# Turning tiles on TensorE by halves of the rows instead of whole, in the local-attention stage of a fused transformer kernel

## The chip, the cores and the metric

The kernel runs on one core of a Trainium2 chip. The metric is the device time of one execution in microseconds, lower being better; of the kernel before three executions were timed.

## The reference, cut to what matters

The program is two small transformer layers and a third part, a local-attention transformer of depth 6, on an input of 4 batches of 512 tokens with 128 features. The first two parts take the first 606 us and aren't touched. The third part is this, for each of its 6 layers:

```python
def attn_layer(x, Wqkv, qs, ksc, Wo):            # 16 heads of 64, window 32
    q, k, v = split(x @ Wqkv)                     # 128 -> 3 * 1024
    q = l2norm(q) * qs;  k = l2norm(k) * ksc      # per head
    q = q * cos * scale + rotate_half(q) * sin * scale
    k = k * cos / scale + rotate_half(k) * sin / scale
    out = local_attention(q, k, v)                # each window of 32 sees itself and the one before
    return out.reshape(b, n, 1024) @ Wo

for i in range(6):
    x = attn_layer(shift_tokens(x), ...) + x
    x = ffn_layer(shift_tokens(x), ...) + x       # layer norm, 128 -> 2 * 341, gelu gate, 341 -> 128
```

In the local attention a query block of 32 tokens meets 64 keys; the scores times 8 are masked, go through a softmax, and weigh 64 rows of v.

## The kernel before, in words

All engines run their own instruction streams and meet at semaphores. The third part walks over tiles of 128 tokens: 6 layers, 4 batches, 4 tiles t = 0 to 3 of a batch, 96 tiles in all. Every engine has a function `slot` that is called once per tile and writes out by hand what the engine does in it; the order on the engine is the order in that function. A slot holds three tiles in different stages: tile g is projected, tile g-1 is turned and scored, tile g-2 is weighted.

On TensorE (`slot`, line 1065) the order is: two query products (`project` 0 and 1, three matmuls of 128x512 each), `turn_q`, key product 2, `probs`, key product 3, values 0, `turn_k`, values 1, value product 4, scores 0, value product 5, scores 1, `out_`. Beside that come parts of the output projection and the feed-forward of earlier batches, by t: in t = 0 the first feed-forward matmuls ahead of `turn_q` and the first half of the output projection (`wo_half`, 16 matmuls with 256 columns) behind it; in t = 1 the second feed-forward matmuls (`ff_down`, line 1167) behind `turn_q`; in t = 2 the second half of the output projection ahead of `turn_q`; in t = 3 a layer norm's turn behind values 1.

The turns are what the change is about. TensorE turns (transposes) the normalised, rotated queries and keys (`ra`), the exponentials (`Ex`) and the weighted values (`On`), each an array of 128 tokens by 1024 columns, in eight blocks of 128 columns, a pair of heads each. A block is a matmul with the data as weights and the identity matrix streaming past them: 128 rows, 128 weight columns, 128 streamed columns. Blocks 0 to 3 go to the first bank of `tr` in PSUM, blocks 4 to 7 to the second (`turn`, `turn_probs`, `turn_out`, lines 1004 to 1025). After every four blocks a semaphore (`qk_tr`, `e_tr`, `on_tr`) tells ScalarE, which copies the bank into SBUF (`take_qk_part`, `take_probs`, `take_out`, lines 2141 to 2165; the profile shows all ScalarE work at line 1924 and all turns at line 589) and counts up `qk_cp`, `pt_cp` or `o_cp`. So the first copy can run while the second four blocks are turned.

Who waits for the copies: scores 0 and values 0 take pairs 0 to 3, so they wait for the first copy of the keys or probabilities (`qk_cp` at `g * 4 + 3`, `pt_cp` at `g * 2 + 1`, lines 1030 and 1046), scores 1 and values 1 for the second. The next turn writes the same banks, so its first four blocks wait for the first copy of the turn before, its second four for the second one. `window_scores` and `values` work with tiles of 64 rows and 32 columns, the two heads of a pair on the two row halves and the four windows on the four column groups, into the two banks of `sc` or `oo` (lines 1027 to 1058).

On VectorE a slot begins, behind the softmax of the tile before, with the rotation of the query products (lines 1729 and 1731), which frees the bank for key product 2. On ScalarE a slot is two squares, the exponential, the query copies (with a gelu between them in t = 0), a square, the probability copies (with a shifted copy of the input between them in t = 1 of most batches), a square, in t = 2 a shifted copy, the mask, the key copies, the value copies, inverse roots, and the output copies (`slot`, line 2172). ScalarE turns to each when it comes to it in that order.

Of the kernel before, what the change touches and what calls it, by code (L numbers as in the profile page):

```python
# [109 lines left out]
def build(nc, ins, out):  # L110
    ctx = ExitStack()
    with ctx:
# [471 lines left out]
        def _(pe):  # L584
# [427 lines left out]
            def turn_probs(g, j):  # L1012

                for u in range(4):
                    pr = 4 * j + u
                    last = tp(tr[:, j, u * P:(u + 1) * P], Ex[:, 2 * pr:2 * pr + 2, :])
                last.then_inc(e_tr, 1)

            def turn_out(g, j):

                pe.wait_ge(on_ok, g + 1)
                for u in range(4):
                    pr = 4 * j + u
                    last = tp(tr[:, j, u * P:(u + 1) * P], On[:, pr * P:(pr + 1) * P])
                last.then_inc(on_tr, 1)
# [39 lines left out]
            def slot(s_):  # L1065
# [10 lines left out]
                def turn_q():  # L1076
                    for j in range(2):
                        if g >= 3:
                            pe.wait_ge(o_cp, (g - 3) * 2 + j + 1)
                        elif g == 2:  # L1080
                            pe.wait_ge(qk_cp, 3 + j)
                        turn(g - 1, t - 1, j)

                def turn_k():
                    for j in range(2):
                        if d_:
                            pe.wait_ge(pt_cp, (g - 2) * 2 + j + 1)
                        else:
                            pe.wait_ge(qk_cp, (g - 1) * 4 + j + 1)
                        turn(g - 1, t - 1, 2 + j)  # L1090

                def probs():
                    pe.wait_ge(e_exp, g - 1)
                    for j in range(2):
                        if c_:
                            pe.wait_ge(qk_cp, (g - 1) * 4 + j + 1)
                        else:
                            pe.wait_ge(o_cp, (g - 3) * 2 + j + 1)
                        turn_probs(g - 2, j)
# [12 lines left out]
                def out_():  # L1112
                    for j in range(2):
                        if c_:
                            pe.wait_ge(qk_cp, (g - 1) * 4 + j + 3)
                        else:
                            pe.wait_ge(pt_cp, (g - 2) * 2 + j + 1)
                        if t == 0 and m2 is not None:
                            pe.wait_ge(ff_ev, m2 * FFC + 2)
                        if t == 3 and j == 0 and m1 is not None:  # L1120
                            pe.wait_ge(lnb_out, m1 + 1)
                        turn_out(g - 2, j)
# [121 lines left out]
            def drain():  # L1244

                for j in range(2):
                    pe.wait_ge(o_cp, (TZ - 2) * 2 + j + 1)
                    turn(TZ, T - 1, j)
# [4 lines left out]
                for j in range(2):  # L1253
                    pe.wait_ge(qk_cp, TZ * 4 + j + 1)
                    turn_probs(TA, j)
                values(NB - 1, TA, T - 2, 0)
                for j in range(2):
                    pe.wait_ge(pt_cp, TA * 2 + j + 1)
                    turn(TZ, T - 1, 2 + j)
# [3 lines left out]
                for j in range(2):  # L1263
                    pe.wait_ge(qk_cp, TZ * 4 + j + 3)
                    turn_out(TA, j)
# [3 lines left out]
                for j in range(2):  # L1269
                    pe.wait_ge(o_cp, TA * 2 + j + 1)  # L1270
                    turn_probs(TZ, j)
# [5 lines left out]
                for j in range(2):  # L1277
                    pe.wait_ge(pt_cp, TZ * 2 + j + 1)
                    turn_out(TZ, j)
# [642 lines left out]
        def _(ac):  # L1922
# [232 lines left out]
            def take_probs(g, j):  # L2155
# [3 lines left out]
                act(PT[:, 4 * j:4 * j + 4, :], tr[:, j].rearrange("p (a b) -> p a b", b=P), ACT.Copy  # L2159
                    ).then_inc(pt_cp, 1)  # L2160

            def take_out(g, t, j):
                ac.wait_ge(on_tr, g * 2 + j + 1)
                act(oT[:, 4 * j:4 * j + 4, t * P:(t + 1) * P], tr[:, j].rearrange("p (a b) -> p a b", b=P),
# [7 lines left out]
            def slot(s_):  # L2172
# [17 lines left out]
                if c_:  # L2190
                    take_qk_part(g - 1, (t - 1) % T, 0)
                if t == 0 and m2 is not None:
                    gelu(m2, 0, FFB[0])
                    log_exp_tables()
                if c_:
                    take_qk_part(g - 1, (t - 1) % T, 1)
# [16 lines left out]
                if d_:  # L2213
                    take_probs(g2, 1)
# [222 lines left out]
```

## Time and profile before

| | |
|---|---|
| median of three executions | 2197.93 us (2195.68 to 2202.28) |
| span of the profiled execution, first to last instruction | 2182.5 us |
| TensorE busy | 2005.7 us, 34395 matmuls |
| VectorE, ScalarE, POOL busy | 1809.4, 1579.9, 1167.3 us |
| stage of the tiles | from 606 us to the end |
| DMA packets of the program, share of 16 engines | 22.0% |

For the profiled execution the profile gives the span; the timed executions hold what lies around it as well, 15.4 us by the median. A matmul's time in the profile is modelled and runs from its issue to its last result, so the starts tell more than the sums. In the timeline, instructions of the same kind in a row are one line: the start of the first, the time from that to the end of the last, and their count.

### The profile page before, as it was taken

The page shows a single profiled execution, that of the slowest core. Times are in us where ns is not written, and L with a number is a line of the kernel's source. Part 1 is how long each engine was busy: PE and PEld are TensorE (multiplying, and loading weights), DVE is VectorE, ACT ScalarE, POOL GpSimd, SP SyncE. Part 2 cuts the span into 40 slices and gives each one's busy share as a digit, 9 for nine tenths or more (in the row PEclk, how much of TensorE's full clock was granted, in tenths as well). Part 3 has the DMA queues.
Part 4 walks back from the last instruction along what each step waited for, and adds up shares of the span by engine and source line. Part 5 has one row for each costly group of instructions (what it writes and reads, how often), then busy time and mean ns, then how long its engine had stood idle before and what let it go on. Part 6 is the DMA issues. An engine that isn't in the chain of part 4 may idle for free.

```text
span 2182.5 us, 82607 instructions
## 1 busy us (share of the span) xinstructions
PE 2005.7 (92%) x34395; PEld 1457.7 (67%) x34395; DVE 1809.4 (83%) x3751; ACT 1579.9 (72%) x3031; POOL 1167.3 (53%) x1413
## 2 busy tenths in 40 slices
PE   6888899987699999999999999999999999999997
PEld 4666654455577776777777777777767777677775
DVE  7888765678798998888988888988888988888884
ACT  4777753365577887787877788777787878887773
POOL 1112110000577676666776667666667767667761
PEclk9999999998899999999999999999999999999999
DMA  4000001000122232222322223322232322332221
GB/s 114 1 2 2 2 31 59 30 1 30 52 72 68 61 105 69 68 63 71 90 72 75 66 58 95 81 68 66 70 87 71 87 58 58 102 82 62 75 59 40
DMA packets 98196, 132.18 MB, mean 61 GB/s; under 512 B 27900, under 2 KB 42882, under 8 KB 97826
## 3 DMA queue, kind: packets, MB, share of 16 engines
q1 hardware_dynamic: 97826, 126.90, 22.0%
q8 instruction: 275, 4.51, 0.8%
q14 instruction: 95, 0.78, 0.1%
HBM read 28.20 MB, written 1.11 MB: 13 GB/s over the span
## 4 chain that ended last, share of the span: by engine, by line
PE 72%; DVE 13%; issue 6%; ACT 6%; POOL 1%; SPq 1%; DMA 0%; DVEq 0%; POOLq 0%; ACTq 0%
PE oo L586 21%; PE pj L586 19%; PE tr L589 14%; PE sc L586 13%; ACT arena L1924 3%; PE tr L586 2%; DVE arena L1729 2%; DVE xn L1318 2%; DVE arena L1486 1%; PE oo L589 1%; DVE arena L1731 1%; DVE arena L1750 1%; DVE arena L1752 1%; PE sc L589 1%; ACT sc L1924 1%
## 5 line engine op out<-in xcount | busy, mean ns | idle before, releaser
L2345 POOL TENSOR_TENSOR arena<-arena 128x1024 f32<-128x1024 f32 x192 | 456.9, 2380 | 336.9 <-DVE arena L1731 336.9
L1924 ACT ACTIVATE arena<-tr 128x512 f32<-128x512 f32 (+2 forms) x874 | 460.8, 570 | 111.9 <-PE tr L589 109.7
L1924 ACT ACTIVATE arena<-pj 128x512 f32<-128x512 f32 x576 | 341.7, 599 | 189.5 <-PE pj L586 150.4
L589 PE MATMUL tr<-ident,arena 128*128 128x128 f32 x2882 | 413.3, 279 | 25.3 <-DMA beta<-in_L_attn_betas 9.8
L1924 ACT ACTIVATE arena<-arena 128x16 f32<-128x16 f32 (+6 forms) x808 | 362.3, 454 | 98.7 <-DVE arena L1486 74.0
L589 PEld LDWEIGHTS tr<-ident,arena 128*128 128x128 f32 x2882 | 330.6, 141 | 93.4 <-issue 34.5
L2363 POOL TENSOR_TENSOR arena<-arena 128x1024 f32<-128x1024 f32 x192 | 366.7, 1910 | 23.2 <-POOL arena L2356 0.9
L1729 DVE TENSOR_TENSOR arena<-pj,rtab 128x512 f32<-128x512 f32 x384 | 259.8, 677 | 24.8 <-ACT arena L1924 23.4
L586 PE MATMUL oo<-slab,arena 64*32 64x64 f32 (+1 forms) x12416 | 232.1, 228 | 41.0 <-issue 26.4
L1731 DVE TENSOR_TENSOR arena<-pj,rtab 128x512 f32<-128x512 f32 x384 | 261.4, 681 | 0.0
L1737 DVE TENSOR_REDUCE arena<-arena 128x8 f32<-128x512 f32 x384 | 255.6, 677 | 0.0
L586 PEld LDWEIGHTS oo<-slab,arena 64*32 64x32 f32 (+1 forms) x12416 | 158.3, 106 | 123.7 <-issue 94.7
L586 PE MATMUL pj<-w_lo,xs_hi 128*128 128x512 f32 x576 | 227.5, 395 | 0.1
L586 PEld LDWEIGHTS sc<-arena 64*32 64x32 f32 x12288 | 136.0, 105 | 91.0 <-issue 75.0
L586 PE MATMUL sc<-arena 64*32 64x64 f32 x12288 | 171.7, 224 | 6.8 <-issue 5.5
L2312 POOL TENSOR_SCALAR rstd<-mv 128x4 f32<-128x4 f32 x40 | 11.4, 284 | 294.3 <-DVE mv L1312 292.2
L1750 DVE TENSOR_REDUCE arena<-sc 128x16 f32<-128x1024 f32 x96 | 117.2, 1220 | 38.5 <-PE sc L586 38.5
L1770 DVE TENSOR_TENSOR slab<-oo,arena 128x1024 f32<-128x1024 f32 x96 | 117.1, 1220 | 18.3 <-PE oo L586 16.2
L1486 DVE CUSTOM_DVE_ANT_0 arena<-pj,biases 128x128 f32<-128x128 f32 (+3 forms) x214 | 101.1, 486 | 24.3 <-PE pj L586 23.2
L586 PEld LDWEIGHTS pj<-w_lo,xs_hi 128*128 128x128 f32 x576 | 110.1, 191 | 16.4 <-issue 12.2
L1752 DVE TENSOR_TENSOR arena<-sc,arena 128x1024 f32<-128x1024 f32 x96 | 117.5, 1224 | 3.3
L1761 DVE TENSOR_REDUCE arena<-arena 128x16 f32<-128x1024 f32 x96 | 116.3, 1212 | 1.0 <-ACT arena L1924 1.0
(289 smaller groups left out, 3802.5 us busy)
## 6 DMA issues: line engine op xcount, KB each, us to landing
slab<-arena SPq DMA_DIRECT2D x576, 128.0 KB, 2.4
slab<-arena SPq DMA_DIRECT2D x336, 64.0 KB, 2.0
wqkv<-in_L_ffn_Wqkv SPq DMA_DIRECT2D x18, 512.0 KB, 4.2
arena<-gate_mem SPq DMA_DIRECT2D x24, 256.0 KB, 4.3
wo<-in_L_ffn_Wo SPq DMA_DIRECT2D x6, 512.0 KB, 4.2
w<-in_L_ffn_W SPq DMA_DIRECT2D x6, 341.0 KB
YT<-in_L_attn_x SPq DMA_DIRECT2D x4, 256.0 KB, 3.5
arena<-in_L_ffn_W SPq DMA_DIRECT2D x1, 1024.0 KB
```

The source lines that it names most:

```text
L586: return nc.tensor.matmul(o, l, r, start=start, stop=stop, **k)
L589: return nc.tensor.transpose(o, i, ident[0:i.shape[0], 0:i.shape[0]])
L1486: v.tensor_tensor_reduce(out=Ssb[:, n % 4, 0:w], in0=SBANK[n % 3][:, 0:w], in1=bias[:, S - w:S], scale=-1.0, scalar=3e38, op0=ALU.add, op1 ...
L1729: v.tensor_tensor(ra[:, t % 2, k, co].rearrange("p (h u d) -> p h u d", u=2, d=DL // 2), src, tc_.unsqueeze(1).broadcast_to(wide), ALU.mult)
L1731: v.tensor_tensor(rb[:, k, co].rearrange("p (h u d) -> p h u d", u=2, d=DL // 2), src[:, :, ::-1, :], ts_.unsqueeze(1).broadcast_to(wide), ...
L1737: v.tensor_reduce(ss[:, k, hf * PAIRS:(hf + 1) * PAIRS, 0], sq[:, c % 2].rearrange("p (h d) -> p h d", d=DL), AX.X, ALU.add).then_inc(ss_o ...
L1750: v.tensor_reduce(mx, s_v, AX.X, ALU.max).then_inc(mx_ok, 1)
L1752: v.tensor_tensor(Tm.rearrange("p (a u) b -> p u a b", u=2), sc[:, :, :].rearrange("p u (a b) -> p u a b", b=2 * WIN), mx.rearrange("p (u ...
L1770: v.tensor_tensor(On.rearrange("p (a u d) -> p u a d", u=2, d=DL), oo[:, :, :].rearrange("p u (a d) -> p u a d", d=DL), ri.rearrange("p (a ...
L1924: return nc.scalar.activation(o, i, f, **k)
L2345: p_.tensor_tensor(r_, r_, rb[:, k, :], ALU.add).then_inc(sum_ok, 1)
L2363: p_.tensor_tensor(r3, r3, rs[:, k, :].unsqueeze(2).broadcast_to([P, HL, DL]), ALU.mult).then_inc(qk_rdy, 1)
```

## The change

A turn is no longer eight blocks of 128 rows but sixteen of 64 rows: for each pair of heads one block takes tokens 0 to 63 into the first bank of `tr`, the next one tokens 64 to 127 into the second. Each has 64 rows, 128 weight columns and 64 streamed columns. A bank then holds all eight pairs of one half of the tokens, and ScalarE's two copies go by halves of the tokens instead of halves of the pairs; their size is the same. The waits of TensorE become one per turn, for the later copy; values 0 and scores 0 wait for both copies. On ScalarE the second copy of the queries now stands directly behind the first, ahead of the gelu of t = 0, and the second copy of the probabilities directly behind the first, ahead of the shifted copy of t = 1 and, once a layer, the conversion of weights. The function `drain` for the last tiles is changed in the same way.

```diff
-            def turn(g, t, j):
-                pe.wait_ge(qk_rdy, g * 2 + j // 2 + 1)
-                for u in range(4):
-                    pr = 4 * (j % 2) + u
-                    last = tp(tr[:, j % 2, u * P:(u + 1) * P], ra[:, t % 2, j // 2, pr * P:(pr + 1) * P])
-                last.then_inc(qk_tr, 1)
...
+            def turn_rows(rows, done):
+                for pr in range(PAIRS):
+                    for u in range(2):
+                        r = slice(u * DL, (u + 1) * DL)
+                        last = nc.tensor.transpose(tr[:, u, pr * DL:(pr + 1) * DL], rows(r, pr), ident[r, r])
+                        if pr == PAIRS - 1:
+                            last.then_inc(done, 1)
+
+            def turn(g, t, k):
+                pe.wait_ge(qk_rdy, g * 2 + k + 1)
+                turn_rows(lambda r, pr: ra[r, t % 2, k, pr * P:(pr + 1) * P], qk_tr)
+
+            def turn_probs():
+                turn_rows(lambda r, pr: Ex[r, 2 * pr:2 * pr + 2, :], e_tr)
+
+            def turn_out(g):
                 pe.wait_ge(on_ok, g + 1)
+                turn_rows(lambda r, pr: On[r, pr * P:(pr + 1) * P], on_tr)

             def window_scores(g, t, i):
-                pe.wait_ge(qk_cp, g * 4 + 3 + i)
                 if i == 0:
+                    pe.wait_ge(qk_cp, g * 4 + 4)
                     pe.wait_ge(masked, g + 1)
...
             def values(n, g, t, i):
-                pe.wait_ge(pt_cp, g * 2 + 1 + i)
+                pe.wait_ge(pt_cp, g * 2 + 2)
...
                 def turn_q():
-                    for j in range(2):
-                        if g >= 3:
-                            pe.wait_ge(o_cp, (g - 3) * 2 + j + 1)
-                        elif g == 2:
-                            pe.wait_ge(qk_cp, 3 + j)
-                        turn(g - 1, t - 1, j)
+                    if g >= 3:
+                        pe.wait_ge(o_cp, (g - 2) * 2)
+                    elif g == 2:
+                        pe.wait_ge(qk_cp, 4)
+                    turn(g - 1, t - 1, 0)
...
                 def probs():
                     pe.wait_ge(e_exp, g - 1)
-                    for j in range(2):
-                        if c_:
-                            pe.wait_ge(qk_cp, (g - 1) * 4 + j + 1)
-                        else:
-                            pe.wait_ge(o_cp, (g - 3) * 2 + j + 1)
-                        turn_probs(g - 2, j)
+                    if c_:
+                        pe.wait_ge(qk_cp, (g - 1) * 4 + 2)
+                    else:
+                        pe.wait_ge(o_cp, (g - 2) * 2)
+                    turn_probs()
...
             def take_qk_part(g, t, j):
                 ac.wait_ge(qk_tr, g * 4 + j + 1)
-                src = tr[:, j % 2].rearrange("p (a b) -> p a b", b=P)
-                pr = slice(4 * (j % 2), 4 * (j % 2) + 4)
-                dst = qT[:, pr, :] if j < 2 else kT[:, pr, WIN + t * P:WIN + (t + 1) * P]
+                src = tr[:, j % 2].rearrange("p (a b) -> p a b", b=DL)
+                at = j % 2 * DL
+                dst = qT[:, :, at:at + DL] if j < 2 else kT[:, :, WIN + t * P + at:WIN + t * P + at + DL]
                 act(dst, src, ACT.Copy).then_inc(qk_cp, 1)
...
                 if c_:
                     take_qk_part(g - 1, (t - 1) % T, 0)
+                if c_:
+                    take_qk_part(g - 1, (t - 1) % T, 1)
                 if t == 0 and m2 is not None:
                     gelu(m2, 0, FFB[0])
                     log_exp_tables()
-                if c_:
-                    take_qk_part(g - 1, (t - 1) % T, 1)
...
                 if d_:
                     take_probs(g2, 0)
+                    take_probs(g2, 1)
                 if s_.ahead is not None and t == 1:
...
-                if d_:
-                    take_probs(g2, 1)
```

`turn_k` and `out_` change as `turn_q` does, `take_probs` and `take_out` as `take_qk_part`.

## Rows read from the trace of the kernel before

**Rows 1.** The page: busy time by engine, and the chain that ended last.
```profile
PE 2005.7 (92%) x34395; PEld 1457.7 (67%) x34395; DVE 1809.4 (83%) x3751; ACT 1579.9 (72%) x3031; POOL 1167.3 (53%) x1413
...
PE 72%; DVE 13%; issue 6%; ACT 6%; POOL 1%; SPq 1%; DMA 0%; DVEq 0%; POOLq 0%; ACTq 0%
```

**Rows 2.** Busy time by engine in the tile stage; then clock, DMA share, GB/s.
```profile
606.00:2150.00 1544.00, 1467.22 (x30311) 1108.26 (x30312) 1342.32 (x2234) 1217.58 (x2242) 1063.97 (x1268) 1.00 0.28 74
```

**Rows 3.** Groups by line and shape on TensorE, from 606 us: busy, mean ns, idle before.
```profile
L589 PE MATMUL tr<-ident,arena 128*128 128x128 f32 x2264 | 301.7, 276 | 4.3 <-POOL arena L2363 2.5 <-ACT arena L1924 1.8
...
L586 PE MATMUL oo<-slab,arena 64*32 64x64 f32 x12160 | 169.4, 224 | 40.7 <-issue 26.2 <-DVE xn L1318 13.6 <-ACT arena L1924 1.0
...
L586 PE MATMUL pj<-wk_hi,xs_hi 128*128 128x512 f32 x186 | 94.4, 507 | 13.7 <-DVE arena L1731 13.7
```

**Rows 4.** Timeline of TensorE in a slot of t = 2: start, length, matmuls, count.
```profile
1514.90 1.04 PE L589 MATMUL tr<-ident,arena 128*128 128x128 f32 x8
1515.69 0.48 PE L586 MATMUL pj<-wk_hi,xs_hi 128*128 128x512 f32 x1
...
1516.24 0.39 PE L586 MATMUL pj<-wk_hi,xs_lo 128*128 128x512 f32 x1
1516.47 1.03 PE L589 MATMUL tr<-ident,arena 128*128 128x128 f32 x8
...
1517.81 0.40 PE L586 MATMUL pj<-wk_hi,xs_lo 128*128 128x512 f32 x1
1518.13 0.86 PE L586 MATMUL oo<-slab,arena 64*32 64x64 f32 x64
1518.92 1.09 PE L589 MATMUL tr<-ident,arena 128*128 128x128 f32 x8
1519.95 0.86 PE L586 MATMUL oo<-slab,arena 64*32 64x64 f32 x64
...
1521.78 0.25 PE L586 MATMUL sc<-arena 64*32 64x64 f32 x3
```

**Rows 5.** Timelines of ScalarE and of TensorE in a slot of t = 0.
```profile
1544.40 0.60 ACT L1924 ACTIVATE arena<-tr 128x512 f32<-128x512 f32 x1 [0.55 <-PE tr L589]
...
1544.64 3.62 PE L586 MATMUL sc<-arena,wo 128*128 128x256 f32 x16
```

**Rows 6.** Timeline of ScalarE in the slot of rows 4 (t = 2).
```profile
1515.53 1.09 ACT L1924 ACTIVATE arena<-tr 128x512 f32<-128x512 f32 x2 [2.29 <-PE tr L589]
...
1517.22 1.08 ACT L1924 ACTIVATE arena<-tr 128x512 f32<-128x512 f32 x2
...
1518.79 1.26 ACT L1924 ACTIVATE xcur<-YT 64x512 f32<-64x512 f32 x2
1520.08 1.03 ACT L1924 ACTIVATE sc<-wmask 128x1024 f32<-128x1024 f32 x1
1521.13 1.08 ACT L1924 ACTIVATE arena<-tr 128x512 f32<-128x512 f32 x2
```

**Rows 7.** Timeline of all engines where a slot of t = 1 begins.
```profile
1493.77 1.28 ACT L1928 ACT_TABLE_LOAD   x1
...
1495.43 1.07 ACT L1924 ACTIVATE arena<-tr 128x512 f32<-128x512 f32 x2
...
1496.07 1.14 PE L589 MATMUL tr<-ident,arena 128*128 128x128 f32 x8
```

**Rows 8.** Timeline of all engines in a slot of t = 3.
```profile
1527.72 1.05 ACT L1924 ACTIVATE arena<-arena 128x1024 f32<-128x1024 f32 x1
...
1528.60 0.50 PE L586 MATMUL pj<-wk_hi,xs_hi 128*128 128x512 f32 x1 [0.59 <-DVE arena L1731]
1528.67 1.08 ACT L1924 ACTIVATE arena<-tr 128x512 f32<-128x512 f32 x2
...
1529.40 1.07 PE L589 MATMUL tr<-ident,arena 128*128 128x128 f32 x8
...
1531.66 0.57 PE L586 MATMUL oo<-slab,arena 64*32 64x64 f32 x35 [0.51 <-DVE xn L1318]
```

More of the change, by code:

```diff
@@ L1002, in project @@
                 mm(pj[:, c % 2], xs_lo[:, x_], w_hi[k][:, w_], start=False).then_inc(pj_mm, 1)
-            def turn(g, t, j):
-                pe.wait_ge(qk_rdy, g * 2 + j // 2 + 1)
-                for u in range(4):
-                    pr = 4 * (j % 2) + u
-                    last = tp(tr[:, j % 2, u * P:(u + 1) * P], ra[:, t % 2, j // 2, pr * P:(pr + 1) * P])
-                last.then_inc(qk_tr, 1)
[L1012 to L1019, printed above, removed]
+            def turn_rows(rows, done):
[11 more added lines that the diff above has]
+            def turn_out(g):
                 pe.wait_ge(on_ok, g + 1)
[L1022 to L1025, printed above, removed]
+                turn_rows(lambda r, pr: On[r, pr * P:(pr + 1) * P], on_tr)
             def window_scores(g, t, i):
-                pe.wait_ge(qk_cp, g * 4 + 3 + i)
                 if i == 0:
+                    pe.wait_ge(qk_cp, g * 4 + 4)
                     pe.wait_ge(masked, g + 1)
@@ L1076, in turn_q @@
                 def turn_q():
-                    for j in range(2):
-                        if g >= 3:
-                            pe.wait_ge(o_cp, (g - 3) * 2 + j + 1)
-                        elif g == 2:
-                            pe.wait_ge(qk_cp, 3 + j)
-                        turn(g - 1, t - 1, j)
-                def turn_k():
-                    for j in range(2):
-                        if d_:
-                            pe.wait_ge(pt_cp, (g - 2) * 2 + j + 1)
-                        else:
-                            pe.wait_ge(qk_cp, (g - 1) * 4 + j + 1)
-                        turn(g - 1, t - 1, 2 + j)
+                    if g >= 3:
[3 more added lines that the diff above has]
+                    turn(g - 1, t - 1, 0)
+                def turn_k():
+                    if d_:
+                        pe.wait_ge(pt_cp, (g - 1) * 2)
+                    else:
+                        pe.wait_ge(qk_cp, (g - 1) * 4 + 2)
+                    turn(g - 1, t - 1, 1)
                 def probs():
                     pe.wait_ge(e_exp, g - 1)
-                    for j in range(2):
-                        if c_:
-                            pe.wait_ge(qk_cp, (g - 1) * 4 + j + 1)
-                        else:
-                            pe.wait_ge(o_cp, (g - 3) * 2 + j + 1)
-                        turn_probs(g - 2, j)
+                    if c_:
+                        pe.wait_ge(qk_cp, (g - 1) * 4 + 2)
+                    else:
+                        pe.wait_ge(o_cp, (g - 2) * 2)
+                    turn_probs()
                 def values_(i):
@@ L1112, in out_ @@
                 def out_():
-                    for j in range(2):
-                        if c_:
[L1115 to L1122, printed above, removed]
+                    if c_:
+                        pe.wait_ge(qk_cp, g * 4)
+                    else:
+                        pe.wait_ge(pt_cp, (g - 1) * 2)
+                    if t == 0 and m2 is not None:
+                        pe.wait_ge(ff_ev, m2 * FFC + 2)
+                    if t == 3 and m1 is not None:
+                        pe.wait_ge(lnb_out, m1 + 1)
+                    turn_out(g - 2)
                 def wo_half(m, i):
@@ L1244, in drain @@
             def drain():
-                for j in range(2):
-                    pe.wait_ge(o_cp, (TZ - 2) * 2 + j + 1)
-                    turn(TZ, T - 1, j)
+                pe.wait_ge(o_cp, (TZ - 1) * 2)
+                turn(TZ, T - 1, 0)
                 pe.wait_ge(v_cp, TZ * 2 + 2)
@@ L1252, in drain @@
                 pe.wait_ge(e_exp, TA + 1)
-                for j in range(2):
-                    pe.wait_ge(qk_cp, TZ * 4 + j + 1)
-                    turn_probs(TA, j)
+                pe.wait_ge(qk_cp, TZ * 4 + 2)
+                turn_probs()
                 values(NB - 1, TA, T - 2, 0)
-                for j in range(2):
-                    pe.wait_ge(pt_cp, TA * 2 + j + 1)
-                    turn(TZ, T - 1, 2 + j)
+                pe.wait_ge(pt_cp, TA * 2 + 2)
+                turn(TZ, T - 1, 1)
                 values(NB - 1, TA, T - 2, 1)
@@ L1262, in drain @@
                 window_scores(TZ, T - 1, 1)
-                for j in range(2):
-                    pe.wait_ge(qk_cp, TZ * 4 + j + 3)
-                    turn_out(TA, j)
+                pe.wait_ge(qk_cp, TZ * 4 + 4)
+                turn_out(TA)
                 final(0)
@@ L1268, in drain @@
                 pe.wait_ge(e_exp, TZ + 1)
-                for j in range(2):
-                    pe.wait_ge(o_cp, TA * 2 + j + 1)
-                    turn_probs(TZ, j)
+                pe.wait_ge(o_cp, TA * 2 + 2)
+                turn_probs()
                 pe.wait_ge(f_cp, 2)
@@ L1276, in drain @@
                 ff_up(MY, 1, LAST_FF[MY][1])
-                for j in range(2):
-                    pe.wait_ge(pt_cp, TZ * 2 + j + 1)
-                    turn_out(TZ, j)
+                pe.wait_ge(pt_cp, TZ * 2 + 2)
+                turn_out(TZ)
                 last_out_project(0)
@@ L2158, in take_probs @@
                     wait(ac, o_mm, g)
-                act(PT[:, 4 * j:4 * j + 4, :], tr[:, j].rearrange("p (a b) -> p a b", b=P), ACT.Copy
+                act(PT[:, :, j * DL:(j + 1) * DL], tr[:, j].rearrange("p (a b) -> p a b", b=DL), ACT.Copy
                     ).then_inc(pt_cp, 1)
@@ L2163, in take_out @@
                 ac.wait_ge(on_tr, g * 2 + j + 1)
-                act(oT[:, 4 * j:4 * j + 4, t * P:(t + 1) * P], tr[:, j].rearrange("p (a b) -> p a b", b=P),
+                act(oT[:, :, t * P + j * DL:t * P + (j + 1) * DL], tr[:, j].rearrange("p (a b) -> p a b", b=DL),
                     ACT.Copy).then_inc(o_cp, 1)
@@ L2191, in slot @@
                     take_qk_part(g - 1, (t - 1) % T, 0)
+                if c_:
+                    take_qk_part(g - 1, (t - 1) % T, 1)
                 if t == 0 and m2 is not None:
@@ L2212, in slot @@
                     weights_high(l, 2)
-                if d_:
-                    take_probs(g2, 1)
                 if new:
```

1 line of the change is left out of this document (removed).

## The prediction

> **What bounds the kernel now.** The page comes first. TensorE is busy 92% of the span and the chain of work that ended last lies on it for 72%, with VectorE next at 13% [rows 1]. The busy table of the tile stage alone (606 to 2150 us) says the same more sharply: TensorE 1467 of 1544 us, VectorE 1342, ScalarE 1218, the granted clock 1.00, which is the upper of its two levels, 2.4 GHz, throughout [rows 2]. The groups by line say what TensorE waits for in that stage: in the values it stands still for 26.2 us that the profile can't put down to anybody and for 13.6 us on a layer norm's `xn`, before the first key product 13.7 us on VectorE's rotation, and before the turns almost nothing [rows 3]. So a tile is a queue of TensorE work with small holes, and what counts is what is added to that queue or taken from it. A tile has four turns (queries, probabilities, keys, output). With 6 layers, 4 batches and 4 tiles there are 96 tiles, 24 of each t, and t matters since other work is slotted in beside the turns.
>
> **Part 1, the turns themselves.** Eight turns of 128x128 take 1.04 us, the modelled time of one being 0.27, so they start (1.04-0.27)/7 = 0.110 us apart [rows 4]. Behind a window product the same eight take 1.09: the first one's weight load of 0.055 is no longer under the work ahead of it. Hence of one turn's 0.110 the load takes 0.055 and the streaming of 128 columns the other 0.055, one after the other.
>
> The new form is 16 turns of 64 rows with 64 streamed columns each. No row shows a 64-row, 128-column tile. The nearest is the window product, 64x32, on eight tiles: 64 of them in 0.86 us [rows 4]. What one column costs there comes from 16 products of 256 columns in 3.62 us [rows 5]: starts (3.62-0.38)/15 = 0.216 apart, 0.38 being an estimate of one's time from the 0.39 of the rows beside it [rows 4]. So each window product has a load of 0.216 x 32/256 = 0.027 and a stream of 0.054 us, 0.081 together, and eight in turn on each of the eight tiles make 0.65, which is what the group takes up to its last start (0.86 less the 0.22 of one [rows 3]). So there the two row halves do stream together, and most loads overlap too. I therefore take the halves as working side by side: eight times 0.055+0.027 = 0.082 us each, first to last start 0.57 against 0.77: **-0.20 us** a turn. Bounds: if a load of half the rows, or a stream, were all there is (0.055 apart on each half), 0.39, so -0.38; if the loads of both halves follow one another, 15 x 0.055 = 0.83, so +0.06.
>
> A rule speaks against the saving. The Trainium skill, "TensorE: Matmul & The Clock Gate", section "LDWEIGHTS (loading the stationary operand)", says that a load goes by its columns and not by its rows. The halved turns then load twice as many columns in all; by it each load stays at its full price, which the sum has, and it leaves open whether two run at once, which is the second rival.
>
> **Part 2, the change of shape.** The product ahead of the values (64x32) starts at 1517.81, and the values 0.32 later, where a turn, of the same shape, comes after 0.23 (1516.24, 1516.47); with its load now exposed that is 0.09+0.055 = **0.15 us** for going in. Coming out, a turn's modelled end lies 0.25 behind the start of the product that follows it (1514.90+1.04 against 1515.69) but only 0.06 behind the start of the values (1518.92+1.09 against 1519.95): 0.19, less the shorter last stream, **0.17 us** [rows 4]. The turn of keys has values on both sides and already pays, and the output's pays going in. Queries, probabilities (both ways) and output (out) are new: five changes of shape in a tile. These two prices are for a change of rows and columns together; the trace has no change of rows alone, so the bounds are 0 and 0.15 / 0.17. I take the upper end, the only row there is.
>
> Here a rule of the Trainium skill decides: "TensorEngine Tiling (Array Packing)", section "Key Properties", says that a change of tiling mode, though not of tile, drains TensorE. By it the upper end holds; without it the sum would be 20 and not 51 us.
>
> **Part 3, the copies.** This is the largest part. Both banks are now filled only at the end of a turn, ScalarE copies one bank after the other, and whoever follows on TensorE needs both copies: values and scores read all pairs over both halves of the tokens, and the next turn writes both banks. Until now the first copy ran under the second half of the turn, and the follower needed the first copy alone. A copy starts about 0.30 us after the start of the matmul that it waits for (the fourth starts at 1514.90+0.33 = 1515.23, the copy at 1515.53 [rows 6]), 0.28 with the shorter stream. The two take 1.09, and TensorE goes on 0.04 later (one copy takes 0.60 [rows 5], and 1495.43+0.60 stands against 1496.07 [rows 7]). New rule: **last start of a turn + 1.41 us**.
> - Probabilities to values: now 1518.13-1517.23 = 0.90 [rows 4], the last start of a turn being its own start plus 1.03 less 0.27; +0.51, in t = 0, 1, 2. A change of shape on the way is inside.
> - Queries to probabilities where one product alone lies between (t = 2): now 1516.47-1515.67 = 0.80 [rows 4], +0.61. In t = 3 the copies run behind the exponential and end at 1528.67+1.08, so the probabilities start at 1529.79 and not 1529.40 [rows 8]. In t = 0 the products of 3.62 us [rows 5] and in t = 1 the feed-forward's second matmuls (line 1167) cover the copies; if that cover went, the +0.61 would be there too.
> - Scores in t = 2: between the probabilities' copies and the keys' copies ScalarE has a square, a shift of 1.26 and the mask of 1.03, from 1517.22+1.08 to 1521.13+1.08 = 3.91 us, while the scores start 3.65 behind the values, on the first copy [rows 4, 6]. They must now wait for the second: +0.26, and the shorter turn of keys saves nothing in front of it.
> - Output to queries, t = 0 into 1: ScalarE is held by a table load, copies at 1495.43 for 1.07, so queries at 1496.54 and not 1496.07: +0.47, with the turn's saving and both changes of shape inside [rows 7].
>
> The two copies that move on ScalarE (the second query copy ahead of a gelu, the second probability copy ahead of the shifted input) delay those by 0.6 us at most; the gelu feeds a gate on VectorE, which the query product of 3.62 us hides. Sizes and layouts of the copies stay, so their 1.09 for two does. SyncE's and POOL's orders aren't touched.
>
> **The sum**, over one set of four tiles. Into t = 1: +0.47. Into t = 2 and into t = 0: output -0.20, out 0.17, in 0.15, so +0.12 each. Into t = 3: nothing, as TensorE waits 0.59 for VectorE in front of the key product [rows 8]. Inside t = 0 and t = 1: three turns -0.60, out 0.17, in 0.15, values +0.51, so +0.23 each. Inside t = 2: two turns -0.40, +0.61, +0.51, +0.26 = +0.98. Inside t = 3: the probabilities' last start is 1529.79+0.055+0.57 = 1530.42, the values follow at 1531.83 and not 1531.66, +0.17, and keys -0.20: -0.03. Together 2.12 us, times 24 = **+51 us**. The profiled execution spans 2182.5 us, so 2233 is expected there; the median of the runs, 2197.93, lies 15 us above that span, which the change doesn't touch: 2249.
>
> **The rivals.**
> - *A change of rows alone doesn't drain.* Then in t = 0, in t = 1, into t = 2 and into t = 0 each lose 0.32: 1.28 x 24 = 31 us less, +20, 2218. For it: every drain in the trace goes with a change of columns. Chance 0.16.
> - *The loads of the halves follow one another.* A turn costs +0.06 instead of -0.20 at the 12 turns of the set that the sum counts: 0.26 x 12 x 24 = +75, so +126, 2324. Against it: 64 window loads of 0.027 would need 1.7 us and take 0.65, though four column groups alone could explain this. Chance 0.20.
> - *Faster.* The place is the spacing on one half. If in half-row tiles the load of the next turn runs under the stream of this one, the spacing is 0.055, a turn saves 0.38, another 0.18 x 12 x 24 = 52 us; without drains that gives 20-52 = -32, 2166. It decides once a turn saves more than 0.20+0.07 = 0.27 us and the drains are free (20/(12 x 24) = 0.07). Against it: today load and stream of a turn stand in line, 0.110. Chance 0.11.
> - *TensorE's lost time is swallowed* by the unexplained pauses in the values (26.2 us [rows 3]), up to half of the 51: 2223, within the range, counted in the forecast's share.
>
> **How the numbers follow.** The forecast has 0.53, the rivals 0.16, 0.20 and 0.11. The prediction is the likeliest case, 2249. The range reaches from below the first rival (2210) to the second (2325); what it leaves out is the faster case and the upper part of the second. A measurement tells 0.3%, 6.6 us, from no change. Faster 0.12; the same 0.05, out of the first rival's and the faster one's edges; slower 0.83.
>
> **What would show it.** In the profile after: the turns' tile form 64*128 with twice the count; a turn's 16 in 0.57 first to last start (0.83 for the second rival, 0.39 for the faster one). The gap from a product to a turn 0.32 and not 0.23, or the first rival holds. ScalarE's two copies in one piece behind every turn, the values 1.41 after the probabilities' last start, and TensorE waits on ScalarE in front of values, probabilities and scores where there are almost none now, some 0.5 us each. Wrong it is if those waits are there and the time isn't, or if TensorE's wait for VectorE's rotation grows instead.

## The result, and the profile after

The changed kernel takes 2240.7 us (median of four executions, 2228.7 to 2246.0) and the kernel before 2199.45 on the same chip: ratio 1.0183, 95% interval 1.0152 to 1.0215, 41 us slower. The forecast was 51 us, 2249.

The page of the changed kernel: spans and busy time, the chain, and three groups.

```profile
span 2244.2 us, 88464 instructions
...
PE 1966.2 (88%) x37467; PEld 1362.4 (61%) x37467; DVE 1801.5 (80%) x3751; ACT 1569.3 (70%) x3031; POOL 1166.4 (52%) x1413
...
PE 64%; DVE 14%; ACT 12%; issue 8%; POOL 1%; SPq 1%; DMA 0%; DVEq 0%; POOLq 0%; ACTq 0%
...
L1009 PE MATMUL tr<-ident,arena 64*128 64x64 f32 x4608 | 205.2, 228 | 32.5 <-ACT arena L1914 28.1
...
L586 PE MATMUL pj<-wk_hi,xs_hi 128*128 128x512 f32 x192 | 100.0, 521 | 24.7 <-DVE arena L1721 24.7
```

TensorE is busy 39.5 us less than before and the execution 62 us longer by its span: the turns got shorter, and what came in their place is waiting. On the chain ScalarE went from 6% to 12% [rows 1]. The turns, in front of which TensorE hardly waited [rows 3], now stand 28 us behind ScalarE's copies. (The first profile of the kernel before was of an execution some 13 us quicker than its median; a second one spans 2196.4 us. The comparison below is by single stretches, and by the second pair of profiles where totals count.)

The same slot as in [rows 4] (t = 2) in the changed kernel, TensorE:

```profile
1545.44 0.71 PE L1009 MATMUL tr<-ident,arena 64*128 64x64 f32 x16
1546.09 0.51 PE L586 MATMUL pj<-wk_hi,xs_hi 128*128 128x512 f32 x1
...
1547.42 0.71 PE L1009 MATMUL tr<-ident,arena 64*128 64x64 f32 x16 [0.36 <-ACT arena L1914]
...
1549.32 0.85 PE L586 MATMUL oo<-slab,arena 64*32 64x64 f32 x64 [0.30 <-issue]
1550.10 0.71 PE L1009 MATMUL tr<-ident,arena 64*128 64x64 f32 x16
1550.74 0.86 PE L586 MATMUL oo<-slab,arena 64*32 64x64 f32 x64
```

The last line but one to [rows 4]'s 1518.92 and 1519.95: from the turn of keys to values 1 it is 0.64 us, not 1.03. But from the turn of queries to that of probabilities it is 1.98, not 1.57, and from there to the values 1.90, not 1.66: there TensorE waits for this (ScalarE, same slot; the pairs of copies are now in one piece each, in [rows 6] too, but start behind the whole turn):

```profile
1546.19 1.09 ACT L1914 ACTIVATE arena<-tr 128x512 f32<-128x512 f32 x2 [2.49 <-PE tr L1009]
...
1548.14 1.08 ACT L1914 ACTIVATE arena<-tr 128x512 f32<-128x512 f32 x2 [0.37 <-PE tr L1009]
```

### The profile page after: what moved, and what is told of

Read it like the earlier page. It is cut to its first block, busy times and chain, and to the rows that moved or that the text cites. A ratio compares the mean times of both kernels' runs of the same rounds, so it can differ in the third digit from the quotient of the medians.

```text
span 2244.2 us, 88464 instructions
## 1 busy us (share of the span) xinstructions
PE 1966.2 (88%) x37467; PEld 1362.4 (61%) x37467; DVE 1801.5 (80%) x3751; ACT 1569.3 (70%) x3031; POOL 1166.4 (52%) x1413
## 4 chain that ended last, share of the span: by engine, by line
PE 64%; DVE 14%; ACT 12%; issue 8%; POOL 1%; SPq 1%; DMA 0%; DVEq 0%; POOLq 0%; ACTq 0%
PE oo L586 21%; PE pj L586 18%; PE sc L586 11%; PE tr L1009 8%; ACT arena L1914 8%; PE tr L586 2%; PE tr L589 2%; DVE arena L1721 2%; DVE xn L1308 2%; DVE arena L1476 2%; DVE arena L1719 1%; PE oo L589 1%; ACT L1918 1%; DVE arena L1740 1%; DVE arena L1742 1%
## 5 line engine op out<-in xcount | busy, mean ns | idle before, releaser
L1914 ACT ACTIVATE arena<-tr 128x512 f32<-128x512 f32 (+2 forms) x874 | 455.2, 569 | 152.2 <-PE tr L1009 143.3
L1009 PEld LDWEIGHTS tr<-ident,arena 64*128 64x128 f32 x4608 | 167.3, 138 | 123.3 <-issue 81.7
L1009 PE MATMUL tr<-ident,arena 64*128 64x64 f32 x4608 | 205.2, 228 | 32.5 <-ACT arena L1914 28.1
L586 PEld LDWEIGHTS sc<-arena 64*32 64x32 f32 x12288 | 141.1, 108 | 119.7 <-issue 91.6
L586 PE MATMUL sc<-arena 64*32 64x64 f32 x12288 | 180.9, 230 | 27.2 <-issue 16.4
L589 PE MATMUL tr<-ident,arena 128*128 128x128 f32 x578 | 104.6, 286 | 20.8 <-DMA beta<-in_L_attn_betas 10.0
L586 PE MATMUL pj<-wk_hi,xs_hi 128*128 128x512 f32 x192 | 100.0, 521 | 24.7 <-DVE arena L1721 24.7
```

Of the source, the lines that this page charges most:

```text
L586: return nc.tensor.matmul(o, l, r, start=start, stop=stop, **k)
L589: return nc.tensor.transpose(o, i, ident[0:i.shape[0], 0:i.shape[0]])
L1009: last = nc.tensor.transpose(tr[:, u, pr * DL:(pr + 1) * DL], rows(r, pr), ident[r, r])
L1914: return nc.scalar.activation(o, i, f, **k)
```

## The experiments

Theory 1 is the forecast's: the wait for both copies costs, the shorter turns give back, the changes of shape (drains) take part of that again. Its rival puts the loss on the drains and on the 6144 added instructions (3072 loads and as many matmuls). Two more theories came up on the way.

**whole_late: the late copies alone.** `turn_rows` of the change with whole blocks, each copy taking four pairs again, all else as in the change:

```diff
-                    for u in range(2):
-                        r = slice(u * DL, (u + 1) * DL)
-                        last = nc.tensor.transpose(tr[:, u, pr * DL:(pr + 1) * DL], rows(r, pr), ident[r, r])
-                        if pr == PAIRS - 1:
-                            last.then_inc(done, 1)
+                    last = tp(tr[:, pr // 4, pr % 4 * P:(pr % 4 + 1) * P], rows(slice(0, P), pr))
+                last.then_inc(done, 2)
```

> Whole blocks of 128 rows as before, but both banks signalled only at the end of a turn, one wait for both copies, and the order of ScalarE's copies as in the change: the late copies alone. Theory 1 (the loss is the wait for both copies): 0.51 at the values in three of four tiles, 0.6 at the probabilities of t = 2, about 0.5 each in front of the queries of t = 1, the probabilities and values of t = 3 and the scores of t = 2, some 3.5 us per set of four tiles, 24 sets: 2275 to 2290 us, slower than the changed kernel, and values 1.44 us behind the last start of the probabilities' turn. Rival (the copies are hidden and the drains and the added instructions cost the time): within 10 us of the kernel before.

Measured: 2273.3 us, 1.0342 of the kernel before (1.032 to 1.0363), **77 us slower**, and 33 slower than the change itself; the 2275 to 2290 expected were just missed. The late copies are the largest term, and the shape gives back some 33 net. A slot of t = 2 in whole_late, TensorE and ScalarE:

```profile
1561.40 1.06 PE L589 MATMUL tr<-ident,arena 128*128 128x128 f32 x8 [0.57 <-ACT arena L1911]
...
1562.50 1.08 ACT L1911 ACTIVATE arena<-tr 128x512 f32<-128x512 f32 x2 [0.76 <-PE tr L589]
...
1562.77 0.40 PE L586 MATMUL pj<-wk_hi,xs_lo 128*128 128x512 f32 x1
1563.69 0.85 PE L586 MATMUL oo<-slab,arena 64*32 64x64 f32 x64 [0.52 <-issue]
```

From the product's last matmul to the values it is 0.92, where [rows 4] have 1518.13-1517.81 = 0.32. The trace books this wait as "issue", since it can't match the copy's signal; the second copy ends at 1562.50+1.08 = 1563.58, 0.11 ahead of the values, so I take it as ScalarE's. The values start 1.50 behind the turn's last start (1.44 expected).

**before_small and after_small: both kernels with small copies.** In the ninth and later tiles each copy takes a sixteenth of its elements, so most of the turned data is left out:

```diff
-                act(dst, src, ACT.Copy).then_inc(qk_cp, 1)
+                n_ = 8 if g >= 8 else None
+                act(dst[:, :, 0:n_], src[:, :, 0:n_], ACT.Copy).then_inc(qk_cp, 1)
```

(4 of 64 instead of 8 of 128 on the changed kernel; the same for `PT` and `oT`.)

> The kernel before with ScalarE's copies of the turned tiles cut to a sixteenth of their elements from the ninth tile on; it leaves out most of the turned data, and serves as the base of after_small. Theory 1: ScalarE stands behind few TensorE waits here, so little is gained, 2175 to 2200 us. Rival (ScalarE is a second bound): below 2150 us.

> The changed kernel with the same cut of the copies, most of the turned data left out: what is left of the change is the shape, five drains and the added instructions in each tile. Theory 1 (turns save 0.28 to 0.33 us each, drains cost 0.12 each): 30 to 45 us below before_small. Rival (drains and instruction loading cost more than the turns save): level with before_small or up to 40 us above it.

Measured: 2186.2 us (0.995 of the kernel before) and 2175.4 (0.9911). ScalarE is no second bound: with a fifth of its work gone the kernel gains 10 us. And with the copies out of the way the new shape is faster, by 11 us in the median (2169.6 to 2186.0 against 2184.1 to 2189.5), so the loss isn't in the shape. But 11 is about a third of the 30 to 45 that theory 1 expected. Something takes back the other 19 to 34 us.

**halves_in_turn: do the row halves run side by side?**

```diff
-                for pr in range(PAIRS):
-                    for u in range(2):
+                for u in range(2):
+                    for pr in range(PAIRS):
```

> The changed kernel with the two loops of a turn swapped: all eight blocks of the upper row half into bank 0, then the eight of the lower one into bank 1, so that two blocks in a row use the same rows. If the two halves' loads and streams run side by side in the change, a turn's first to last start goes from 0.49 to 1.0 or more, the first copy starts half a turn ahead of the end, and the time is 2245 to 2300 us. If the spacing is set by something else than the rows, the turn stays at 0.49 and the earlier copy brings the time below 2230 us.

Measured: 2282.9 us (1.0387, 1.0365 to 1.041), 42 above the change. The turn of the probabilities in a slot of t = 1, with its two copies:

```profile
1548.91 1.01 PE L1009 MATMUL tr<-ident,arena 64*128 64x64 f32 x16
...
1549.66 1.09 ACT L1914 ACTIVATE arena<-tr 128x512 f32<-128x512 f32 x2
```

It takes 1.01 and not 0.71, from first to last start 0.79 and not 0.49; 1.0 or more was expected. The single starts say why (medians over the turns of the stage, 377 and 378). In the change the sixteen blocks start as eight pairs, 3 ns apart within a pair, and from pair to pair 0.111 us once and then 0.062. In halves_in_turn the starts fall into two rows of eight of just that spacing, 0.111 and then 0.062: the first half's, and from 0.304 on the second half's, which begin while three of the first half are still to come. So eight blocks on one half take 0.484 from first to last start, and sixteen on both take 0.487: **the halves run fully side by side**. And one half alone is quicker than the 0.082 that I had added up. The first step is longer than the others by its exposed load, 0.049; with whole blocks it is 0.055 (0.164 against 0.109), so a load of half the rows costs nearly the full price. By an estimate from these, 0.062-0.049 = 0.013 us of the 0.027 of streaming is left beside the next load and the rest hides under it, where with 128 rows load and stream stand in line (0.109).

A half by itself thus takes as long as both together, and handing over the first bank early gains nothing: in both kernels the first copy starts 0.81 us behind the turn's start and the second 1.30 (medians).

**keys_halves and its companions: the half of the change that should pay.** The turn of keys has window products on both sides, so no drain is added, and over a microsecond of work lies ahead of the scores. Only this turn is halved, by the change's own loop; the scores wait for both copies. In keys_halves_mask_first ScalarE also does this in t = 2, and in before_mask_first nothing else is changed:

```diff
-                if t == 2 and m1 is not None:
-                    ac.wait_ge(y_att, m1 * 2 + 2)
-                    shifted(xsF, YT[:, s_.y1:s_.y1 + S], 0, S).then_inc(xs_f, 1)
                 if c_:
...
                     take_qk_part(g - 1, (t - 1) % T, 3)
+                if t == 2 and m1 is not None:
+                    ac.wait_ge(y_att, m1 * 2 + 2)
+                    shifted(xsF, YT[:, s_.y1:s_.y1 + S], 0, S).then_inc(xs_f, 1)
```

> The kernel before with the turn of keys alone by row halves: it has window products on both sides, so it adds no change of shape, and over a microsecond of other work lies between it and the scores. Theory 1 (turn saves 0.33, drains and late copies are what the change loses by): -0.33 in t = 0, 1 and 3; in t = 2 the scores wait for the second copy, 0.47 more, less what is saved: about -0.5 us per set, 2180 to 2192 us beside a kernel before at 2197. Rival (the added instructions alone cost more than the turns save): level or slower.

> As keys_halves, and in t = 2 ScalarE does the mask and the key copies ahead of the shifted input instead of behind it, so that the scores need not wait for the second key copy. Theory 1: -0.33 in all four tiles and the 0.15 that the scores of t = 2 waited: -1.4 us per set, 2155 to 2172 us. Rival (VectorE bounds once TensorE is shorter, its wait before the key product grows): no faster than keys_halves.

> The kernel before with that order of ScalarE alone. Theory 1: removes the 0.15 us that the scores of t = 2 waited for the first copy, some 4 us, 2190 to 2197. Rival (the order is what brings the gain and the halved turn nothing): as fast as keys_halves_mask_first.

Measured: 2222.6 us (1.0112, 1.0099 to 1.0126), 2215.2 (1.0078, 1.0058 to 1.0098) and 2198.2 (1.0001, 0.9992 to 1.0011). All three expectations of theory 1 failed: the turn of keys is 0.39 us shorter in 96 tiles, 37 us, and the kernel is 25 us *slower*. In keys_halves_mask_first TensorE's waits for ScalarE in front of the scores are 1.9 us instead of the 12.2 of keys_halves, which accounts for the 7 us between the two. Where the rest goes the trace shows. keys_halves, TensorE, early in the stage:

```profile
666.56 0.71 PE L1010 MATMUL tr<-ident,arena 64*128 64x64 f32 x16
667.20 0.72 PE L586 MATMUL oo<-slab,arena 64*32 64x64 f32 x49
669.67 0.34 PE L586 MATMUL oo<-slab,arena 64*32 64x64 f32 x15 [1.74 <-issue]
...
670.83 1.15 PE L586 MATMUL sc<-arena 64*32 64x64 f32 x64
...
673.25 0.63 PE L586 MATMUL pj<-w_lo,xs_hi 128*128 128x512 f32 x1
673.67 0.63 PE L586 MATMUL pj<-wv_hi,xs_lo 128*128 128x512 f32 x1
```

Two things. First, 1.74 us of standstill in the midst of a group whose instructions wait for nothing. Between 666.5 and 669.7 us the DMA engines carry one packet, and it is this:

```profile
q8 instruction: 1, 0.02, 2.4%
```

A packet of instructions is 16 KB (4.60 MB in 281 packets), and from pause to pause the matmuls counted in the trace are multiples of 126 or so: a packet holds 256 instructions, a load and a matmul being two. TensorE resumes a median of 2.4 to 2.6 us after such a packet starts. I read this as TensorE having run out of instructions. Second, after the pause two matmuls of 512 columns start 0.42 us apart and not 0.23. The stages by window, columns as in [rows 2]:

```profile
663.00:670.80 7.80, 6.06 (x167) 4.69 (x165) 5.62 (x11) 6.52 (x11) 4.51 (x2) 1.00 0.08 20
670.80:674.20 3.40, 3.40 (x72) 2.48 (x71) 2.51 (x10) 0.92 (x3) 1.79 (x5) 0.52 0.02 5
674.20:680.00 5.80, 5.19 (x92) 4.25 (x92) 4.95 (x9) 4.98 (x10) 4.94 (x8) 0.99 0.36 93
```

For 3.4 us the granted clock is at its lower level, 1.2 GHz; ahead of it came the turn, then the pause. The kernel before shows 1.00 in the whole stage [rows 2].

**more_instructions and the padded pair: is it the count of instructions, or how fast they are used?** Theory 2: in the stretch from values to scores TensorE uses up instructions faster than packets of them arrive. First 3072 instructions were added (the page's count goes from 82607 to 85679; I had reckoned with 6144) that do no work:

```diff
+            def passed():
+                for _ in range(8):
+                    pe.wait_ge(set_tr, 1)
```

called at the head of `turn`, `turn_probs` and `turn_out`. Then work with few instructions was added to the kernel before and to keys_halves:

```diff
+                if c >= 4:
+                    mm(pj[:, c % 2], xs_hi[:, x_], w_hi[k][:, w_])
                 mm(pj[:, c % 2], xs_hi[:, x_], w_hi[k][:, w_], stop=False)
```

> The kernel before with eight further waits on a semaphore passed long ago ahead of each half turn, 64 a tile, 6144 in all, about as many instructions as the change adds on TensorE. If the pauses in the midst of window products come from loading instructions, their total rises from some 40 us towards 60 and the time by 15 to 30 us beyond what the waits take themselves; if they come from something else, they stay at 37 to 43 us.

> The kernel before with the first matmul of each value product done once more ahead of it: two matmuls of 512 columns a tile, 0.23 us each, 4 instructions in all, 96 tiles: 44 us of streaming, in the stretch of the window products. Theory 2 (in that stretch TensorE is held by the loading of its instructions, 16 KB at a time, each 2.4 us from its start to the next instruction): part of it falls into the pauses, whose total drops from 43 towards 30 us: 2215 to 2235 us. Theory 1 alone: the pauses stay, 2235 to 2245.

> The same padding on keys_halves (2222.6 us, pauses of 84 us). Theory 2: the pauses shrink by half or more of what is added, to 40 to 60 us, and the padding costs 10 to 25 us only: 2232 to 2248 us, so that the distance to before_padded is smaller than the 25 us without padding, or gone. Theory 1 alone: the full 44 us, 2262 to 2270, the pauses staying at 84.

Measured: 2248.6 us (1.0228, 1.0213 to 1.0243), 2221.7 (1.0114, 1.0094 to 1.0134) and 2244.2 (1.0213, 1.0198 to 1.0228). The added instructions cost 51 us by themselves, but the pauses, which were to stay or to grow, shrink to 30 us: the count isn't it. (The page has 287 packets of instructions for 275, twelve more for its 3072 instructions, which is 256 in each.) The padding of 44 us costs 24 us in the kernel before and 22 in keys_halves, so half of it falls into time that was lost anyway: the pauses are 7 to 12 and 17 us shorter. That much of theory 2 holds. That the two would close up failed: they stay 22 us apart, the pauses of keys_halves_padded being 64 us and not 40 to 60.

**before_again and after_again: a second look at both.** Theory 3: with half-row turns go two costs, pauses and falls of the clock.

> The kernel before once more, for a second profile of it: its first one spans 2182.5 us, 13 less than the median. Theory 3 (two costs go with half-row turns: pauses at the loading of instructions, and falls of the granted clock to its lower level): pauses of 37 to 47 us, at most three falls of the clock between 606 us and 35 us before the end. Rival (the first two profiles differ by chance): either is as large as in the changed kernel.

> The changed kernel once more. Theory 3: pauses of 50 to 70 us and ten or more falls of the clock, 35 to 50 us at the lower level, 2235 to 2246 us. Rival: pauses and falls as in the kernel before, with the time still 40 us above it.

Measured: 2195.3 us and 2235.4 (ratio 0.9986 and 1.017, 1.0143 to 1.0197). The falls came out as theory 3 has them; the pauses of before_again, 48 us, lie just above the expected 37 to 47. All runs side by side. A pause is counted where two matmuls of one group and of fewer than 512 columns, the second waiting for nothing, start more than 0.4 us apart; a fall is a stretch at 1.2 GHz in the trace's record of the clock, from 606 us to 35 us before the end. The last column counts the standstills of TensorE of 1.3 us or more, by the ends of its matmuls, for whatever reason.

| kernel | median us | pauses, their us | falls, us at 1.2 GHz | standstills of 1.3 us and more |
|---|---|---|---|---|
| before | 2199.5 | 45, 43 | 0, 0 | 3 |
| before_again | 2195.3 | 49, 48 | 3, 10 | 8 |
| before_mask_first | 2198.2 | 46, 45 | 1, 3 | 6 |
| before_padded | 2221.7 | 34, 36 | 2, 7 | 6 |
| before_small | 2186.2 | 46, 40 | 4, 14 | 8 |
| more_instructions | 2248.6 | 36, 30 | 0, 0 | 6 |
| whole_late | 2273.3 | 39, 38 | 2, 7 | 5 |
| *half-row turns:* the change | 2240.7 | 54, 64 | 13, 48 | 22 |
| after_again | 2235.4 | 51, 56 | 11, 44 | 14 |
| after_small | 2175.4 | 65, 67 | 7, 34 | 17 |
| halves_in_turn | 2282.9 | 44, 49 | 11, 48 | 13 |
| keys_halves | 2222.6 | 68, 81 | 11, 41 | 24 |
| keys_halves_mask_first | 2215.2 | 74, 86 | 10, 44 | 18 |
| keys_halves_padded | 2244.2 | 48, 64 | 10, 41 | 24 |

The falls separate the two families without an exception, 0 to 4 against 7 to 13. The sum of the pauses doesn't explain it: halves_in_turn has the pauses of before_again and 11 falls to its 3. The single long standstills may. Each of the 85 falls has a standstill of TensorE of 1.2 to 2.9 us right beside it, one that still lasts when the clock falls or has ended at most 2.2 us before, be it a pause or a wait for another engine; and of standstills of 1.3 us and more the half-row kernels have 13 to 24, the others 3 to 8. Not each brings a fall: 68 of 132 do in the half-row kernels, 11 of 42 in the others. So whether the half-row turns count by themselves, or only through the longer standstills that come with them, no run here separates.

The views show the same where totals are given, the stretch from 606 to 2150 us of before_again and of after_again having a granted clock of 1.00 and 0.99:

```profile
606.00:2150.00 1544.00, 1461.54 (x29885) 1.00 0.28 73
```

```profile
606.00:2150.00 1544.00, 1390.80 (x32332) 0.99 0.28 72
```

The waits of TensorE in after_again and then in before_again:

```profile
PE oo L586 <- issue: 53.5, 89, 2.6
PE tr L1009 <- ACT arena L1914: 26.4, 71, 0.7
PE pj L586 <- DVE arena L1721: 22.2, 25, 1.0
...
PE sc L586 <- ACT arena L1914: 9.9, 17, 0.6
```

```profile
PE oo L586 <- issue: 28.2, 27, 2.5
PE pj L586 <- DVE arena L1731: 13.6, 23, 0.6
```

(89 "issue" waits for 27: ScalarE's late copies in front of the values are booked there, as in whole_late, beside the pauses.)

## Why the prediction was right, point by point

The time came out near, 2240.7 us for 2249, and the mechanism of the loss is the forecast's, but that the sum fits is in part luck. Interval by interval, in us from start to start, forecast and measured (after_again less before_again, medians of the 23 or 24 slots of each t, behind values 1 the lower quartile, since many pauses fall there):

| interval | t = 0 | t = 1 | t = 2 | t = 3 |
|---|---|---|---|---|
| output to queries | +0.12, -0.08 | +0.47, +0.48 | +0.12, -0.08 | 0, -0.09 |
| queries to probabilities | +0.12, -0.04 | +0.12, -0.15 | +0.41, +0.40 | +0.39, +0.39 |
| probabilities to values 0 | +0.31, +0.27 | +0.31, +0.27 | +0.31, +0.25 | -0.22, -0.02 |
| values 0 to scores 0 | -0.20, -0.40 | -0.20, -0.36 | +0.26, +0.11 | -0.20, -0.38 |
| together | +0.35, -0.25 | +0.70, +0.25 | +1.10, +0.68 | -0.03, -0.10 |

The other intervals differ by 0.01 at most. Where a copy decides, the forecast is met within 0.06 us (0.15 in front of the scores); the values of t = 3 wait for VectorE's layer norm instead (17.3 us over the run for 13.5). Where the turn and its changes of shape decide, the kernel is 0.09 to 0.27 quicker than forecast. The set of four tiles comes to 0.58 us and not 2.12, so **14 us and not 51**. The other 26 of the 40 between the two runs are no term of the forecast.

- **The bound, and the late copies.** Right, and nearly to the size: the last start of the probabilities' turn is 1547.42+0.71-0.22 = 1547.91, the values follow 1.41 us later, as forecast. From the queries' last start, 1545.44+0.49, to the probabilities it is 1.49 (1.41 forecast). In front of the scores of t = 2 TensorE waits 0.58 us and starts 3.76 behind the values (3.91 forecast, 3.65 in [rows 4]). By itself the part costs 77 us, as whole_late shows, or 88 (3.66 a set) by the same intervals, the pauses of whole_late being 10 us shorter than those of before_again.
- **The change of shape.** Drains are there, and the first rival is out, but they are cheaper than the forecast took from the window products. A turn that a product follows takes 0.64 us to that product's start, its own first to last start being 0.49, so 0.15 for going out, where the kernel before has 0.03 (median of the single starts): **0.12, not 0.17**. Going in is 0.09 later by start (0.32 for 0.23), with the exposed load's 0.049 within the turn's own time: 0.14, nearly the 0.15 forecast. By the Trainium skill, "TensorEngine Tiling (Array Packing)", section "Key Properties", a change of tiling mode drains TensorE; the trace agrees, and a change of the rows alone is enough for it.
- **The turns.** The term that was mis-sized most: 0.28 us saved by first to last start between products (0.49 for 0.77), not 0.20, and 0.39 behind window products, since the way from the turn to values 1 goes from 1.03 to 0.64. At fault is the spacing within one half, put at 0.055+0.027 = 0.082 and measured as 0.062: part of the stream hides under the next load, the faster rival's mechanism, though it counted on all of it (0.055). That the halves work side by side, which the forecast took from the window products, holds in full. So the second rival, loads one after the other and 0.83 from first to last start, is out.
- **What was left out.** Pauses at the loading of instructions, which I had seen as 26.2 us of "issue" [rows 3] and only counted on to swallow losses; and the clock. They make good the too small saving, which is why the sum came out near. An account by stretches: late copies +77 (whole_late). Shape: keys 0.39, output to product 0.85-0.64 = 0.21, queries and probabilities 0.79-0.64-0.09 = 0.06 each: 0.72 x 96 = -69 (14-88 = -74 by the intervals); in t = 3 some goes into VectorE's wait (0.91 us there where [rows 8] have 0.59; 22.2 for 13.6 us over the run). Clock: 34 us more at half speed, at most 17 us of work. Pauses: 8 to 21 us more. Together +33 to +46 with the clock at its most, measured 41. The last two are counted and not isolated, so how they share the rest stays open.
- **keys_halves** goes by the same account: keys -37, the scores' wait for the second copy (12 us on ScalarE in its waits), pauses 81 against 48, +33, clock 31 us more at half speed, up to +15: +23, measured 25.
- **What lies around the span.** I put the difference between the first profile and the median down to the time around the span. Wrong: in the profiled execution of the change that is 1.8 us (2245.97 against 2244.2); the profile of the kernel before was of a quick execution.

With half rows each bank holds all pairs, so the first bank can be handed over early only if its half is turned first. That is halves_in_turn: in 185 of 378 turns the first copy starts ahead of the turn's last block, and nothing is gained, for the reason given there. No version that computes the whole result beat the kernel before; after_small is faster and leaves out most of the copying.

## What to carry to other kernels

Before a unit of work is cut so that both PSUM banks fill at the same time, count what the earlier hand-over of the first bank was worth: here two copies of 0.54 us behind the turn instead of one beside it cost 77 us, more than the turns gave. And a stretch of small matmuls can be bound by the loading of its instructions: look for "issue" idle in the midst of a group, and for a packet of instructions on the DMA at that time; where it is there, making the matmuls in between faster can move time into pauses, as it did in keys_halves.

## What the runs showed that was not expected

- 64-row, 128-column turns: one block each 0.062 us on one half alone, two each 0.062 with the halves alternating, against 0.109 for a whole block with twice the streamed columns.
- TensorE pauses of up to 3.1 us from one start to the next where a 16 KB packet of instructions comes in, 2.4 to 2.6 us from the packet's start to the next instruction; 43 to 48 us in all in the kernel before, 81 and 86 us where only one turn in four was made shorter.
- With half-row turns the granted clock fell to 1.2 GHz 7 to 13 times in the stage for 34 to 48 us in all; without them 0 to 4 times. Each fall stands beside a standstill of TensorE of 1.2 to 2.9 us. What else the chip goes by in this the runs don't show.
- Eight waits on a long-passed semaphore ahead of each half turn cost 51 us. The page counts 3072 more instructions, half of the 6144 that the code writes: about 0.017 us for each that it counts.
